# Self-attention's slots, the normalising, the last key products of a batch and the first shared units, each moved in a Perceiver block

## The reference

```python
def stablemax(x):
    s = jnp.where(x >= 0, x + 1.0, 1.0 / (1.0 - x))
    return s / jnp.sum(s, axis=-1, keepdims=True)
...
k = key_value @ Wk.T + bk
v = key_value @ Wv.T + bv
...
scores = jnp.einsum('bhqd,bhkd->bhqk', q, k) / np.sqrt(HD)
attn = stablemax(scores)
context = jnp.einsum('bhqk,bhkd->bhqd', attn, v)
...
x = x + L0_xattn(layernorm(x), ctx_1024, ...)   # 64 queries, 1601 keys
x = x + L0_attn(layernorm(x), ...)              # causal, 8 query heads, one key/value head
x = x + L0_ffn(layernorm(x), ...)               # 2 shared experts, 8 routed, top 2, exact gelu
```

## Time and profile before

| | |
|---|---|
| runs | 1239.51, 1241.25, 1242.89 us |
| median | 1241.25 us |
| profiled execution, its own time | 1241.11 us, span 1239.4 us |
| TensorE busy | 1210.2 us, 98% |
| VectorE, ScalarE, POOL busy | 839.8, 687.0, 571.7 us |
| chain that ended last | TensorE 91%, VectorE 4% |
| DMA | 179.40 MB, mean 145 GB/s |

### The profile page before, as it was taken

One profiled execution on the slowest core, in us unless ns is written; L12 is line 12 of the kernel. 1 busy time (PEld: TensorE's weight loads), 2 busy tenths in 40 slices (PEclk: granted clock), 3 DMA queues, 4 the chain that ended last, 5 costly groups with the idle time before them and its releaser, 6 DMA issues.

```text
span 1239.4 us, 33792 instructions
## 1 busy us (share of the span) xinstructions
PE 1210.2 (98%) x14478; PEld 1133.6 (91%) x14478; DVE 839.8 (68%) x1265; ACT 687.0 (55%) x1236; POOL 571.7 (46%) x357
## 2 busy tenths in 40 slices
PE   8999999999999999999999998999999999999998
PEld 7899999989999989999989997898889999999997
DVE  7666786776777686786785875766676455555655
ACT  4366656745755655756656557555644445544443
POOL 5656767776758776867766764000041001000000
PEclk9999999999999999999999998899999999999999
DMA  7331111121121212012112123745455599999991
GB/s 268 121 105 40 41 40 37 44 73 67 41 82 39 76 70 70 23 67 74 41 70 74 36 107 146 306 172 179 170 191 208 192 362 345 346 338 354 355 384 36
DMA packets 34794, 179.40 MB, mean 145 GB/s; under 512 B 6264, under 2 KB 9496, under 8 KB 15568
## 3 DMA queue, kind: packets, MB, share of 16 engines
q1 hardware_dynamic: 32896, 172.42, 38.0%
q0 software_dynamic: 1744, 4.76, 1.2%
HBM read 168.97 MB, written 8.19 MB: 143 GB/s over the span
## 4 chain that ended last, share of the span: by engine, by line
PE 91%; DVE 4%; issue 2%; POOL 1%; ACT 1%; DMA 0%; DVEq 0%; SPq 0%; POOLq 0%
PE bank L928 18%; PE bank L931 18%; PE bank L1285 12%; PE sc L1302 9%; PE sc L951 7%; PE sc L1146 7%; PE bank L970 4%; PE sc L1166 4%; PE bank L1166 4%; PE bank L909 1%; PE bank L1037 1%; DVE tt L1623 1%; POOL xn L731 1%; PE bank L1091 1%; PE bank L996 1%
## 5 line engine op out<-in xcount | busy, mean ns | idle before, releaser
L731 POOL TENSOR_TENSOR xn<-xn,tt 128x1024 f32<-128x1024 f32 x96 | 231.9, 2416 | 165.1 <-DVE tt L1623 163.3
L931 PE MATMUL bank<-wvh,blk 128*128 128x256 f32 x1344 | 248.8, 287 | 5.3 <-DVE va L1594 5.3
L928 PE MATMUL bank<-blk,wkh 128*128 128x256 f32 x1344 | 246.0, 285 | 0.0
L1721 DVE TENSOR_TENSOR wsl<-ring,wsh 128x2048 fp32r<-128x2048 f32 x72 | 165.2, 2294 | 112.6 <-ACT wsh L1378 109.8
L1442 ACT ACTIVATE tt<-sc 128x512 f32<-128x512 f32 (+1 forms) x208 | 107.8, 603 | 217.1 <-PE sc L951 209.3
L931 PEld LDWEIGHTS bank<-wvh,blk 128*128 128x128 f32 x1344 | 209.9, 192 | 8.8 <-DVE va L1594 6.1
L928 PEld LDWEIGHTS bank<-blk,wkh 128*128 128x128 f32 x1344 | 209.2, 192 | 4.2 <-issue 1.6
L931 PE MATMUL bank<-wvl,blk 128*128 128x256 f32 x672 | 190.6, 284 | 0.0
L928 PE MATMUL bank<-blk,wkl 128*128 128x256 f32 x672 | 190.0, 283 | 0.0
L1378 ACT CAST wsh<-ring 128x2048 fp32r<-128x2048 f32 x72 | 137.4, 1909 | 45.8 <-PE sc L1302 21.2
L1285 PEld LDWEIGHTS bank<-xT,ring 128*128 128x128 f32 x1280 | 144.8, 192 | 1.0
(11 more groups left out here) (327 smaller groups left out, 2204.9 us busy)
## 6 DMA issues: line engine op xcount, KB each, us to landing
ring<-in_w SPq DMA_DIRECT2D x112, 1024.0 KB, 6.1
stg<-in_ctx SPq DMA_DIRECT2D x24, 1024.0 KB, 5.0
wqt<-in_wo SPq DMA_DIRECT2D x4, 1024.0 KB, 5.0
wqt<-in_aq SPq DMA_DIRECT2D x4, 1024.0 KB, 5.0
wqt<-in_ap_ SPq DMA_DIRECT2D x4, 1024.0 KB, 4.9
yrows<-K SPq DMA_DIRECT2D x1, 2048.0 KB, 12.4
bsum<-in_tails SPq DMA_DIRECT2D x2, 520.0 KB, 6.6
ktail<-bsum SPq DMA_DIRECT2D x1, 1040.0 KB, 4.1
```

The source lines that it names most:

```text
L731: e.tensor_tensor(dacc[0:kn, y, :], dacc[0:kn, y, :], tt[0:kn, w, :], ALU.add).then_inc(s["da_pool"], 1)
L928: m = e.matmul(dst[:, 256 * a:256 * a + 256], w[:, WPOS[j], c, r], x[:, c, :], start=(k_ == 0), stop=(k_ == 5))
L931: m = e.matmul(dst[:, 256 * a:256 * a + 256], x[:, c, r], w[:, WPOS[j], c, :], start=(k_ == 0), stop=(k_ == 5))
L1721: e.tensor_tensor(wsl[m % 3][:], ring[slot(unit_split(m))][:], wsh[m % 3][:].bitcast(F32), ALU.subtract).then_inc(s["wl_dve"], 1)
```

## The change

1. **Products.** In the third part of each batch but the last, slot 11 makes three products of the next keys and slot 12 two, where it was two and three.
2. **ScalarE.** In slot 10 the high part of block 6 is made after the logarithms and exps of the pair, where it stood before them.
3. **Self-attention.** Every step of tiles 0 to 2 comes four slots later: output, rows and turn in r = 10, 11 and 12, queries, keys and scores in r = 0, 1 and 2 of the next batch, and so on. The split of the output weights now comes three slots ahead of step 0 (r = 7 on ScalarE, 8 on POOL), and again in step 6.
4. **Normalising.** The first half of the heads stays four slots behind the batch's last slot (r = 3), the second half comes six behind it (r = 5).
5. **The passage.** The low part of unit 0 moves from the head of slot 100 to its end. Unit 2's high part is now made by VectorE at the end of slot 100 and its low part at the head of slot 102's weights (`weights_second`), counted by a semaphore of its own; ScalarE no longer makes it. In slot 102 the weights of chunk 101 come with those of chunk 102. Up 1 moves to slot 102, behind up 0, and up 2 to slot 104.
6. **Names.** The three banks are numbered 7, 0, 1 in place of 0, 1, 7, and the waits of `positions` and of the tail's values are renumbered to fit. These parts and the renumbered waits for `wl_dve` are left out below.

```diff
--- before.py
+++ after.py
@@ -80,7 +80,7 @@
     if i == NPART - 1:
         v, k = ((0, 3), (3, 5), (5, 6), (6, 7), (7, 7))[d], (0, 0)
     elif i % PER_BATCH == PER_BATCH - 1:
-        v, k = ((0, 3), (3, 6), (6, 7), (7, 7), (7, 7))[d], ((0, 0), (0, 0), (0, 2), (2, 4), (4, 7))[d]
+        v, k = ((0, 3), (3, 6), (6, 7), (7, 7), (7, 7))[d], ((0, 0), (0, 0), (0, 2), (2, 5), (5, 7))[d]
     else:
         v, k = ((0, 4), (4, 7), (7, 7), (7, 7))[d], ((0, 0), (0, 0), (0, 4), (4, 7))[d]
     return [("v", i, j) for j in range(*v)] + [("k", i + 1, j) for j in range(*k)]
@@ -107,8 +107,8 @@
             den.append(b)
             if last:
                 nrm.append((b, 0, 4))
-        if lag == 4 and not last:
-            nrm += [(b, 0, 2), (b, 2, 2)]
+        if lag in (4, 6) and not last:
+            nrm.append((b, lag - 4, 2))
     return den, nrm
 
 
@@ -120,7 +120,7 @@
 
 def halved(slot, what):
 
-    return next((t for t in range(3) if slot == (slot_of(t, 0) - 5, slot_of(t, 5))[what]), None)
+    return next((t for t in range(3) if slot == (slot_of(t, 0) - 3, slot_of(t, 6))[what]), None)
 
 
 def slot_of(t, d):
@@ -129,7 +129,7 @@
         return NCH + 2 + LAST_TILE[d]
     if t == 2 and d == 14:
         return NCH
-    return 2 * PER * t + 2 * PER + 6 + (9 if d == 10 else d)
+    return 2 * PER * t + 2 * PER + 10 + (9 if d == 10 else d)
 
 
 def tile(slot, d):
...
@@ -378,7 +378,7 @@
         ring_in = [st.enter_context(nc.semaphore(f"ring{i}_in")) for i in range(NR)]
         b1_in = [st.enter_context(nc.semaphore(f"b1_{k}_in")) for k in range(NBLK)]
 
-        pj = [bank[0], bank[1], bank[7]]
+        pj = [bank[7], bank[0], bank[1]]
         uses = projections()
         use = {u: n for n, u in enumerate(uses)}
         pob = bank[6]
@@ -418,6 +418,13 @@
         def unit_split(m):
 
             return m if m < 32 else unit_routed(*divmod(m - 32, 4), 1)
+
+        def wait_split(e, m):
+
+            if m == 2:
+                e.wait_ge(s["first_dve"], 2)
+            else:
+                e.wait_ge(s["wl_dve"], m + (m < 2))
 
         def slot(n):
             return n % NR
...
@@ -1226,11 +1233,9 @@
                 if tile(n, 9) is not None:
                     for b in range(2):
                         attended(tile(n, 9), b)
-                if n == NCH - 1:
-                    shared_up(1)
                 for m in group_before(n):
                     weighted(m)
-                if NCH + 1 < n < NCH + 2 * NSH:
+                if NCH + 2 < n < NCH + 2 * NSH:
                     shared_up(n - NCH)
                 if tile(n, 2) is not None:
                     turn_rows(tile(n, 2))
@@ -1242,6 +1247,9 @@
                     product(*made_)
                 if n == NCH - 2:
                     shared_up(0)
+                    shared_up(1)
+                if n == NCH:
+                    shared_up(2)
                 if n == PLACE:
                     positions()
                 if n == PLACE + 2:
...
@@ -1441,8 +1449,6 @@
                     for hb in range(2):
                         e.activation(weights_view(m, kn, hb), score_read(m, kn, hb), ACT.Relu,
                                      scale=-1.0).then_inc(s["t_act"], 1)
-                if d == 2 and last and i + 1 < NPART:
-                    context_hi(i + 1, 6)
                 for m in group(n):
                     w, kn = m % TR, tokens(m)
                     for hb in range(2):
@@ -1453,6 +1459,8 @@
                         r = slice(512 * hb, 512 * hb + 512)
                         e.wait_ge(s["ln_act"], 2 * m + hb + 1)
                         e.activation(tt[0:kn, w, r], tt[0:kn, w, r], ACT.Exp, scale=-1.0).then_inc(s["ex_act"], 1)
+                if d == 2 and last and i + 1 < NPART:
+                    context_hi(i + 1, 6)
                 if d == 1 and i + 1 < NPART:
                     for j in ORDER[:6]:
                         context_hi(i + 1, j)
@@ -1474,9 +1482,7 @@
                     weights_hi(1)
                 if NCH <= n < NCH + 2 * NSH:
                     gelu(n - NCH)
-                    if n == NCH:
-                        weights_hi(2)
-                    elif n - NCH + 2 < 32:
+                    if NCH < n < NCH + 30:
                         weights_hi(n - NCH + 2)
                 if tile(n, 5) == 3:
                     for half in range(2):
@@ -1717,9 +1723,21 @@
                 e.tensor_tensor(gates[:, t, :], pj_of("g", t)[:, 0:8], rbt[:], ALU.add).then_inc(read_of("g", t), 1)
 
             def weights_split(m):
-                e.wait_ge(s["wh_act"], m + 1)
+                e.wait_ge(s["wh_act"], m + (m < 2))
                 e.tensor_tensor(wsl[m % 3][:], ring[slot(unit_split(m))][:], wsh[m % 3][:].bitcast(F32),
                                 ALU.subtract).then_inc(s["wl_dve"], 1)
+
+            def weights_second(lo):
+
+                if lo:
+                    e.wait_ge(s["v_pe"], PROD * NPART)
+                    e.wait_ge(s["first_dve"], 1)
+                    m = e.tensor_tensor(wsl[2][:], ring[slot(2)][:], wsh[2][:].bitcast(F32), ALU.subtract)
+                else:
+                    e.wait_ge(ring_in[slot(2)], ring_value(2))
+                    e.wait_ge(s["v_pe"], PROD * NPART - 5)
+                    m = e.tensor_copy(wsh[2][:], ring[slot(2)][:])
+                m.then_inc(s["first_dve"], 1)
 
             def hidden(s_):
                 e.wait_ge(s["ge_act"], s_ + 1)
@@ -1926,8 +1944,6 @@
                 last = i % PER_BATCH == PER_BATCH - 1
                 if n % PER == 0 and 0 < n <= NCH:
                     batch_sums(n // PER - 1)
-                if n == NCH - 4:
-                    weights_split(0)
                 if n == NCH - 1:
                     weights_split(1)
                 if d == 0 and i + 1 < NPART:
@@ -1976,18 +1992,24 @@
                 before = ((2, 1, 2, 1, 1) if last else (2, 0, 2, 0))[d]
                 for p_ in products(n)[:before]:
                     joined(*p_)
+                if n == NCH - 2:
+                    weights_second(1)
+                    weights(n - 1, 0)
+                    weights(n - 1, 1)
                 for m in group(n - 1)[1:] + group(n)[:1]:
-                    weights(m, 0)
-                    weights(m, 1)
+                    if m != NCH - 3:
+                        weights(m, 0)
+                        weights(m, 1)
                 for p_ in products(n)[before:]:
                     joined(*p_)
                     if p_ == ("v", i, 4) and i + 1 < NPART:
                         context_sum(i + 1, 3)
+                if n == NCH - 4:
+                    weights_split(0)
+                    weights_second(0)
                 for b, g, m in finished(n)[1]:
                     normalised(b, g, m)
 
-                if n == NCH + 1:
-                    weights_split(2)
                 if NCH <= n < NCH + 2 * NSH:
                     hidden(n - NCH)
                     if n > NCH and n - NCH + 2 < 32:
```

20 lines of the change are left out of this document (10 added, 10 removed).

## The result

The changed kernel takes 1254.58 us (median of 5 runs, 1250.54 to 1256.93) against 1240.91 before: a ratio of 1.0107, 95% interval 1.0085 to 1.0129. The profiled execution took 1255.37 us against 1241.11. The forecast was 1240.1 us, no difference.

The account below looks back on a forecast made before the run. TensorE, busy 98%, bounds the kernel, so only its idle or half-clock stretches count. Main stage 14.3 come, 12.9 go (1.4 slower), passage 2.5 faster: 1241.11 to 1240.0, median 1240.1 us; range 1232.5 to 1247.5.

Parts of the forecast that it names:

- term E: Slot 5, batches 1 to 6: short normalising steps meet POOL's low parts, fourth key product waits 0.87 each, 5.2 us lost.
- the move of self-attention: Output-weight split and half the normalising leave the old place: 5.3 us of value waits and 1.5 of half clock gone.
- The waits that go: Main stage: tail-score waits of 0.54 and 1.32 (6.1 us) and value waits of 1.75 (5.3 us) disappear.
- A: Scores behind batches 0, 1, 3 and 5 wait 1.2 each for VectorE's two-operation join and tail's weights: 4.8 us lost.
- B: Turn in slot 12 of batches 2, 4 and 6 waits 1.2 each for POOL's normalised rows: 3.6 us lost.
- C: Query copy, now in slot 0: 0 to 0.2 each, 0.2 us lost in all.
- D: POOL's 4.63 us split in slot 8 delays VectorE's context sums: taken at 0.5 us lost.
- rival 2: Clock falls behind each A and in full behind the passage's 2.15 wait: 7.5 us lost, 1247.6 us, slower; chance 0.12.
- The passage: Passage to the shared units: 11.6 us of waits and clock removed, 7.5 of waits added; 2.5 us faster after clock allowance.
- the 1.75: Value-product wait, three times, ascribed to VectorE's ten normalising steps in a row, one at 2.00 beside the 4.63 split.
- a rival's ground: Rival 3, slot 5: full lock through POOL's operations adds 1.3 to 2.8 in each of six batches, 1248 us; chance 0.11.

Follow-up runs that it names:

- n9: Kernel before with the passage changed, products 3 + 2, and in slot 12 the tail's weights ahead of both joins on VectorE: 1235.36 us, ratio 0.9962; again 1233.7.
- n15: Changed kernel with ScalarE's high part of block 6 ahead of the exps again (part 2 undone alone): 1246.65 us, ratio 1.0059.
- n1: Changed kernel with both halves of the normalising again four slots behind the batch (part 4 undone alone): 1247.59 us, ratio 1.0062.
- n18: Kernel before with only self-attention's new slots, its output weights' splits and the passage (parts 3 and 5): 1244.09 us, ratio 1.0036.
- n20: Changed kernel with part 2 undone, the normalising halves together, and the tail's weights ahead of both joins in slot 12: 1238.54 us, ratio 0.9985.
- n4: Kernel before with the passage to the shared units alone changed (part 5): 1236.53 us, ratio 0.9971.
- n21: n9 with POOL's output-weight split in slot 4, made to wait for VectorE's third context sum: 1227.41 us, ratio 0.9890.

## Why the prediction was wrong

The step that failed most is the clock: the sum had 1.5 us gained in the main stage, and 10.2 were lost there. Half of this came with two waits of 2.93 that the sum did not have, since it took term E to be the same in each of batches 1 to 6. And the move of self-attention, priced as a gain, is a loss.

- **The waits that go:** right, all ten are gone, though for another reason than the one given (below).
- **A, behind a batch:** 1.14 four times for 1.2, right in place, cause (n9) and size. **B, the turn:** 1.30, 1.27, 1.27 for 1.2, right as well; n15 shows that in this order of products B was part 2's.
- **E, the half in slot 5:** the mechanism was right. In batches 1, 2, 4 and 6 the steps took 5.8 us behind the reciprocal where I took 4.3, and the fourth key product waited 1.14 for 0.87. What failed is "in each of batches 1 to 6": in batches 3 and 5 the attended products, moved into slot 6, hold two of the three banks until VectorE has come past the half, and the second key product waits 2.93. n1 gives E, with its clock, as 6 to 7 us; the sum had 5.2.
- **The move of self-attention:** I had priced it by what leaves the old slots (5.3 and 1.5 of gain) and two small terms, C and D. D was 2.0 and not 0.5, and POOL's second split, moved as well, had no term at all. n18 puts the move alone at 8 us of loss, n20 with the repairs at 3. In both, 5 us of the main stage are in no wait of over 0.4 and in no fall of the clock, and stay open.
- **The clock:** that was rival 2, given 0.12. Its price of 7.5 was near, but its time, 1247.6, is 7 us short. Its condition was wrong: it put the limit between 1.32 and 1.75, and the clock fell behind two of the four A and behind both waits of 2.93, 5.1 us each. What the counts above show is a chance that goes with length and place.
- **The passage:** right, 2.5 taken and 2.5 to 3.6 measured (n4).
- **The cost of a wait:** at the four key products of E it was 0.25 over the idle time, 1.0 in all, which I left out.

The ground for the 1.75 was misread. The prediction has ten steps in a row as its cause, with the second step at 2.00 beside the split of 4.63. But that split was over at 251.06, and the step began at 254.06. Beside it ran POOL's sums, held back by the split, and the step ended 0.16 behind them (timeline of the kernel before):

```profile
251.02 4.88 POOL L731 TENSOR_TENSOR xn<-xn,tt 128x1024 f32<-128x1024 f32 x2
```

One step of 0.29 that took 2.00 made nearly the whole wait of 1.75. n1, n18 and n21 have the ten steps together and no wait there, so part 4 was not needed.

By terms, for a main stage that was forecast 1.4 longer and measured 18.7: the clock 10, the two waits of 2.93 4.1, the values 1.5, the four 0.25s 1.0, and A, B and E together 1. These make 17.5 for a miss of 17.3, and the sum is good to 1 or 2 us: where the granted clock gives 1.7 or 3.4 us lost, the landmarks give about 1.5 or 3.0.

The Trainium skill's rule that VectorE and GpSimd share their SBUF interfaces (GPSIMD Engine Reference, 1. Specifications), and that this is an exclusive lock (Trainium Architecture — The Big Picture, What this means for kernel authors), agrees with 3.33 beside 4.58 and with 0.29 alone. It was weighed in the prediction as a rival's ground and should have been the term's base: with every short step ending behind a POOL operation, E's five steps come out at 6.8 in batch 1, as measured.

## What to carry to other kernels

Before a step is moved, write down what every engine issues for it and what each of them is doing at that place, not at the head of the slot; POOL's long operations count twice, for POOL's queue and for every short SBUF operation of VectorE beside them. A wait that only keeps POOL's long operation off such a stretch can be worth more than the move itself. And price a new idle time of TensorE at more than its length. Here one of 2.6 us or more brought the clock down nearly always, one of 1.7 to 2.1 every second time and one of 1.14 between never and every third time, by its place; each fall behind a wait of up to 3.1 cost 1.5 to 3 us.

## What the runs showed of the hardware

- A short VectorE operation on SBUF that met a POOL operation ended only behind it, however long (0.29 of work took 3.33 beside 4.58, a context sum of 0.68 took 4.86 beside 4.60), and the copy with rounding (one input) waited like those with two (1.20 for 0.23). Reciprocals (0.94) and joins that read PSUM (0.69) kept their time beside POOL.
- TensorE's granted clock fell to 1.2 GHz behind idle times as short as 0.50 (3 of 15 at the scores), and stayed at 2.4 GHz behind all 36 of 1.2 to 1.5. At 2.6 and more it fell 26 times in 28. Where it fell behind a wait of up to 3.1, 1.7 or 3.4 us of granted clock were lost, and nothing between. The same place can fall in one execution and not in the next (562 in the changed kernel). That would fit the spread of 6 us over the changed kernel's runs, but only one execution of each group was traced.
